# Attention inputs of a four-layer graph network as single 32-row products of blocks of 8 by 16 nodes

## The chip, the core and the metric

One NeuronCore of a Trainium2 chip. The time is device microseconds of one execution, median of the runs; all data are float32 and start and end in the chip's memory (HBM).

## What is computed

128 graphs of 64 nodes with 128 features, and a weighted, sparse adjacency `adj` (128, 64, 64), pass through four layers, each with a layer norm and relu ahead and a residual. Layer 0 is a filter network over all pairs; layers 2 and 3 are graph convolutions. The change touches layer 1, hyperbolic attention over all 64 x 64 pairs of a graph, cut here to what matters:

```python
h = proj(mobius_add(proj(mobius_matvec(W, x)), hyp_bias))
x_loc  = clip(logmap(h[:, :, None, :], h[:, None, :, :]), -1000, 1000)   # (b, i, j, d)
x_self = logmap(h, h)
q = concatenate([broadcast(x_self over j), x_loc], axis=-1)
a = silu(q @ att_w1.T + att_b1)
adj_att = sigmoid(a @ att_w2.T + att_b2)[..., 0]                         # (b, i, j)
support = sum over j of adj_att[..., None] * x_loc * mask[..., None]
t = concatenate([x_self, support], axis=-1)
out = silu(t @ mlp_w1.T + mlp_b1) @ mlp_w2.T + mlp_b2 + x_self           # then expmap, logmap0, silu, expmap0
```

`logmap(h_i, h_j)` is a combination of h_i and h_j with two scalars per pair. So what goes into the silu for a pair (i, j) is, per feature, V(i,j) times row j of one projection of h, plus U(i,j) times row i of the same projection, plus row i of another one. These are the three pair terms.

## The kernel before

Three stages follow one another with a barrier of all engines between them: set-up, the filter stage (layer 0) and the flow stage (layers 1 to 3). Nodes lie on partitions, two graphs to a tile of 128 nodes; eight tiles make a group, and there are eight groups.

The flow stage is software-pipelined by hand. Time is counted in slots of 64 ticks; `run` (line 760) emits each engine's instructions by the tick that is written beside each step. In slot s the attention of group s is done, one set of 2048 pairs every two ticks, a tile every eight. Beside it run four chains: `lead` (group s+2: layer 0's output, layer norm, hyperbolic map), `pair` (group s+1: the scalars U, VT and VP of all pairs, and the projections), `mix` (group s-1: sum over neighbours and the rest of layer 1) and `last` (group s-2: layers 2 and 3). All engines take their instructions strictly in order, so a wait holds up all that stands behind it on that engine.

A set in attention:
- `inputs(s)` on PE (lines 997 to 1015): for each of four blocks c, which are row groups of 32 partitions and write PSUM bank c, a product of 512 columns with `HW` (the projected rows of 32 nodes j) against `VD`, then one with `OWN` (two projections of 16 nodes i) against `UD`, added in the same bank. Every float32 matmul shows as two loads and two passes in the trace. Before block 0 PE waits for the first silu of the set before, before block 2 for the second.
- two silus on ACT (`silu`, line 1164), each over two banks, into `SI`.
- `dots(s)` on PE (line 1017): the product with `att_w2`, emitted one set behind, into bank 7. After 32 sets ACT's `weights` makes the group's attention of them.

Where the right sides come from: `VD` is made by POOL (`neighbours`, line 1318), half a tile at a time into three buffers, as VT spread over a mask. `UD` holds U on a block diagonal and ones; it lies in HBM in templates, made in set-up and copied 15 times in the filter stage; SP stores U of a group into it with 8 DMAs (line 946) and loads it for each tile.

SP issues all DMAs, in one order. `load_rows(tile)` (line 898, at ticks 1, 9, 17, ... for the tile after the present one) waits until the tile before the present one is through and issues 7 DMAs: 1 `HW`, 4 `OWN`, 2 `UD`, into two buffers. At tick 9 of `mix` (line 950) it loads the adjacency and `fH`, waits for the attention, stores it, waits for the store, and loads it back as 8 DMAs into `fat` (line 965). At tick 33 of `pair` (line 935) it stores the projections: 1 DMA to `hw` and 16 to `own`. At tick 49 it stores U. `last` and `lead` have some more at ticks 33 and 9. On DVE, `lead` may centre the next group (`bXC`, tick 35.9) only after those stores are through.

## Time and profile before

| | us |
|---|---|
| median of 3 runs (2820.68 to 2827.33) | 2826.15 |
| the profiled execution, its own time | 2826.92 |
| its span, first to last instruction | 2824.9 |
| PE busy, matmul (share of the span) | 2575.6 (91%) |
| DVE busy | 2198.6 (78%) |
| ACT busy | 2162.7 (77%) |
| POOL busy | 1704.4 (60%) |
| DMA, mean rate | 155 GB/s |

The filter stage takes the first half of the span, the flow stage the second; its slots last 132 to 152 us. Rows of the trace give start and length of an instruction, or of several of one kind that lie together (x8). Matmuls overlap, so their lengths don't add up: how far apart they begin is what counts. SP's DMA rows are the time in which SP issues, not the transfer.

### The profile page before, as it was taken

How to read it: one execution, taken by the hardware profiler on the slowest of the kernel's cores; microseconds unless marked ns; L12 is line 12 of the kernel's file. 1: busy time of each engine (PE TensorE's matmuls, PEld its weight loads, DVE VectorE, ACT ScalarE, POOL GpSimd, SP SyncE). 2: the span in 40 equal slices, each digit the busy share in tenths (PEclk: the TensorE clock that was granted, in tenths of full speed). 3: DMA queues.
4: the chain of work that ended last, by engine and by line, in shares of the span. 5: the costliest groups of instructions: out<-in, count | busy, mean ns of one | idle time of the engine just before them, and what ended most of it. 6: DMA issues, size and time to landing. Idle time of an engine off the chain costs nothing. (4 is left out here: it accounts for less than half of the span.)

```text
span 2824.9 us, 53482 instructions
## 1 busy us (share of the span) xinstructions
PE 2575.6 (91%) x21008; PEld 1077.0 (38%) x21008; DVE 2198.6 (78%) x3639; ACT 2162.7 (77%) x2136; POOL 1704.4 (60%) x773
## 2 busy tenths in 40 slices
PE   4899999999999999999962999999999999999963
PEld 2333333333333333333332334344443435343433
DVE  6698998989989899898978365768687878774356
...
GB/s 235 183 224 245 237 255 247 205 196 202 196 196 202 194 199 202 195 198 197 180 38 70 96 126 131 106 115 115 116 123 127 117 118 126 116 120 109 94 45 19
DMA packets 247241, 438.99 MB, mean 155 GB/s; under 512 B 86752, under 2 KB 212320, under 8 KB 213344
## 3 DMA queue, kind: packets, MB, share of 16 engines
...
## 5 line engine op out<-in xcount | busy, mean ns | idle before, releaser
L691 POOL TENSOR_TENSOR f_gate<-rfT,f_sq 128x1024 f32<-128x1024 f32 x512 | 1218.3, 2380 | 226.6 <-DVE f_prod L706 151.6
L624 PE MATMUL PS<-f_h,w_W2T 64*64 64x512 f32 x8192 | 998.4, 591 | 9.7 <-PE PS L624 1.9
L706 DVE SCALAR_TENSOR_TENSOR f_prod<-PS,b2l,f_gate 128x1024 f32<-128x1024 f32 x512 | 657.3, 1284 | 146.3 <-PE PS L624 110.4
L1164 ACT ACTIVATE a_silu<-PS,c_att_b 128x1024 f32<-128x1024 f32 x512 | 543.1, 1110 | 247.3 <-PE PS L1012 246.5
L586 ACT ACTIVATE f_h<-PS,c_b 128x1024 f32<-128x1024 f32 x512 | 556.6, 1113 | 166.6 <-PE PS L606 165.9
L698 DVE TENSOR_REDUCE yT<-f_prod 128x16 f32<-128x1024 f32 x512 | 618.7, 1209 | 0.0
L1324 POOL TENSOR_TENSOR a_vd<-n_vt,jmask 128x1024 f32<-128x1024 f32 x128 | 255.9, 2000 | 543.2 <-PE PS L1012 543.2
L624 PEld LDWEIGHTS PS<-f_h,w_W2T 64*64 64x64 f32 x8192 | 340.5, 133 | 561.4 <-issue 435.9
L606 PE MATMUL PS<-f_gauss,W1two 64*64 64x512 f32 x4096 | 545.8, 594 | 7.4 <-ACT f_gauss L573 4.8
L1008 PE MATMUL PS<-a_vd,a_hw 32*128 32x512 f32 x2048 | 397.6, 656 | 52.0 <-ACT a_silu L1164 24.8
L1012 PE MATMUL PS<-a_ud,a_own 32*128 32x512 f32 x2048 | 367.9, 603 | 0.0
L1027 PE MATMUL PS<-a_silu,w2sel 128*32 128x512 f32 x2048 | 278.0, 615 | 19.3 <-ACT a_att L1170 18.3
L606 PEld LDWEIGHTS PS<-f_gauss,W1two 64*64 64x64 f32 x4096 | 170.0, 133 | 287.5 <-issue 276.1
L568 ACT ACTIVATE f_gauss<-f_gauss,c_off 128x2048 f32<-128x2048 f32 x126 | 252.2, 2002 | 0.0
L573 ACT ACTIVATE f_gauss<-f_gauss 128x2048 f32<-128x2048 f32 x128 | 237.6, 1904 | 0.7
L1008 PEld LDWEIGHTS PS<-a_vd,a_hw 32*128 32x128 f32 x2048 | 127.1, 187 | 239.5 <-ACT a_silu L1164 127.7
L1012 PEld LDWEIGHTS PS<-a_ud,a_own 32*128 32x128 f32 x2048 | 155.3, 190 | 102.5 <-issue 97.6
L1027 PEld LDWEIGHTS PS<-a_silu,w2sel 128*32 128x32 f32 x2048 | 40.5, 108 | 193.8 <-issue 164.5
L573 ACT ACT_TABLE_LOAD x64 | 82.1, 1283 | 5.9 <-PEq L138 4.7
L586 ACT ACT_TABLE_LOAD x64 | 82.1, 1283 | 1.2
L1411 DVE TENSOR_TENSOR b_small<-b_small 128x8 f32<-128x8 f32 (+1 forms) x272 | 76.2, 280 | 8.3
L1283 ACT ACTIVATE f_lh<-f_x,g_small 128x128 f32<-128x128 f32 x128 | 52.1, 484 | 28.6 <-DVE g_small L1411 28.6
...
## 6 DMA issues: line engine op xcount, KB each, us to landing
f_gauss<-in_adj SPq DMA_DIRECT2D x128, 1024.0 KB, 11.7
f_sq<-adj_sq SPq DMA_DIRECT2D x256, 512.0 KB, 10.0
a_ud<-ud_d SPq DMA_DIRECT2D x128, 512.0 KB, 6.3
a_own<-own_d SPq DMA_DIRECT2D x256, 64.0 KB, 1.9
...
```

The lines of the kernel that those rows point to most:

```text
L573: A.activation(half_of(tile, h), half_of(tile, h), ACT.Exp, scale=COEFF).then_inc(s_gauss, 1)
L586: A.activation(H[n % H_BUFS][:], pre(n % 2), ACT.Softplus, bias=cols["b1"][:]).then_inc(s_ssp, 1)
L606: PE.matmul(pre(done % 2)[r, b, :], W1two[rows[b], r], G[tile % G_BUFS][rows[b], part * BANK:(part + 1) * BANK], start=True, stop=True).th ...
L624: PE.matmul(post("message", c)[rows[b], n, :], W2T[rows[k], rows[fh]], hidden(c, n)[rows[k], b, :], start=not second, stop=bool(second)).t ...
L691: GP.tensor_tensor(by_pair(GATE[c % GATE_BUFS][:]), rf, by_pair(squares), ALU.mult).then_inc(s_gate, 1)
L698: V.tensor_reduce(yT[:, fh, first:first + CHUNK // NODES], by_pair(PR[c % PR_BUFS][:]), AX, ALU.add).then_inc(s_sum, 1)
L706: V.scalar_tensor_tensor(PR[c % PR_BUFS][:], post("message", c).rearrange("p b n -> p (b n)"), b2l[:, c % 2:c % 2 + 1], GATE[c % GATE_BUFS ...
L1008: PE.matmul(PS[:, c, :], HW[n][rows_of(c), :], VD[s // 2 % VD_BUFS][rows_of(c), i % 2 * BANK:(i % 2 + 1) * BANK], start=True, stop=False)
L1012: last = PE.matmul(PS[:, c, :], OWN[n][rows_of(c), i, :], UD[n][rows_of(c), i * BANK:(i + 1) * BANK], start=False, stop=True)
L1027: last = PE.matmul(PS[part:part + 32, Z_BANK, :], w2sel[:, 32 - lane:64 - lane], SI[(2 * s + c // 2) % SI_BUFS][:, c % 2 * BANK:(c % 2 + 1 ...
L1164: A.activation(SI[p % SI_BUFS][:], PS[:, first:first + 2, :].rearrange("p b n -> p (b n)"), ACT.Silu, bias=cols["att_b1"][:]).then_inc(s_s ...
L1324: GP.tensor_tensor(VD[part % VD_BUFS][:].rearrange("p (i m) -> p i m", m=32), VT[tile // GT % 2][:, tile % GT, k * 2 * BLOCK:(k + 1) * 2 * ...
```

## The change

A set still has 2048 pairs, but a block of 32 partitions now covers all three pair terms at once, for 8 nodes i by 16 nodes j: 16 rows of projected j, 8 rows of the first projection of i and 8 of the second. So the two products of 512 columns per block become four products of 128 columns with no addition in PSUM, each with its own weights (`ROWS`), 16 matmuls per set for 8. The right side, `OUTER`, is made by POOL in two instructions per set out of two tables in SBUF, `BY_I` (by node i: VT, or fixed masks) and `BY_J` (by node j: U, or fixed masks), two sets ahead in four buffers. Each group's VT and U go straight from SBUF into these tables, with 8 and 32 DMAs. The rows of a tile come with 16 DMAs (8 of them broadcast j rows) in place of 7; the projections are stored with 4 DMAs of 512 KB in place of 17; the attention comes back with 16 DMAs in place of 8. The templates, their store in set-up and 15 copies in the filter stage go. Four activations at the start of the flow stage write the masks into the tables. Some tiles of `mix` and `last` now lie in `yT`. DVE's and PE's waits follow the new counts. The core of the diff:

```diff
@@ -553,9 +546,6 @@
                     load_squares(n)
-            if COPIES_FROM <= tile < COPIES_FROM + len(templates) - 1:
-                SP.dma_start(templates[tile - COPIES_FROM + 1], templates[0]).then_inc(s_copied, 16)
-        SP.wait_ge(s_copied, 16 * (len(templates) - 1))
         SP.wait_ge(d_later, 16 * LATER_WEIGHTS)
...
@@ -720,7 +710,8 @@
 N_FIRST, N_BANKS, Z_BANK = 4, 3, 7
-SI_BUFS, VD_BUFS, RING = 4, 3, 2
+SI_BUFS, OUTER_BUFS, OUTER_AHEAD = 4, 4, 2
+A_BLOCKS = NODES // A_BLOCK
 HALF_GT = GT // 2
...
@@ -794,24 +785,25 @@
     number = fill_numbers()
-    HW = [sb(f"a_hw{n}", [P, P]) for n in range(2)]
-    OWN = [sb(f"a_own{n}", [P, BLOCKS, P]) for n in range(2)]
-    UD = [sb(f"a_ud{n}", [P, PAIRS // 2]) for n in range(2)]
-    VD = [sb(f"a_vd{n}", [P, CHUNK]) for n in range(VD_BUFS)]
+    ROWS = [sb(f"a_rows{n}", [P, A_BLOCKS, 2, P]) for n in range(2)]
+    BY_I = [sb(f"a_by_i{n}", [P, 2, GT, NODES]) for n in range(2)]
+    BY_J = [sb(f"a_by_j{n}", [P, GT, A_BLOCKS, 2, BLOCK]) for n in range(2)]
+    OUTER = [sb(f"a_outer{n}", [P, 2, BLOCK, BLOCK]) for n in range(OUTER_BUFS)]
     SI = [sb(f"a_silu{n}", [P, CHUNK]) for n in range(SI_BUFS)]
     VP = [sb(f"n_vp{n}", [P, GT, NODES]) for n in range(3)]
-    VT = [sb(f"n_vt{n}", [P, GT, NODES]) for n in range(2)]
+    VT = sb("n_vt", [P, GT, NODES])
-    fXC, fSQ, fH, fST, fUU, fAV, fBT, gH, gU = (sb("f_" + n, [P, GT, P]) for n in
-                                               ("xc", "sq", "h", "st", "uu", "av", "abt", "lh", "lu"))
-    fat, fam, ftm = (sb("f_p" + n, [P, GT, NODES]) for n in ("at", "am", "tm"))
+    fXC, fSQ, fH, fST, fUU, fAV, fBT = (sb("f_" + n, [P, GT, P]) for n in ("xc", "sq", "h", "st", "uu", "av", "abt"))
+    gH, gU = (yT[:, n, 0:GT * P].rearrange("p (t d) -> p t d", d=P) for n in range(2))
+    fam = sb("f_pam", [P, GT, NODES])
+    fat, ftm = (yT[:, n, GT * P:GT * P + GT * NODES].rearrange("p (t d) -> p t d", d=NODES) for n in range(2))
     BS, FS = sb("b_small", [P, len(B_ROWS), GT]), sb("f_small", [P, len(F_ROWS), GT])
...
@@ -899,17 +898,17 @@
             if tl == 0:
-                SP.wait_ge(d_hw, (g + 1) * 16)
-                SP.wait_ge(d_own, (g + 1) * 16 * 16)
-                SP.wait_ge(d_u[g % 2], (g // 2 + 1) * 8 * 16)
-            SP.dma_start(HW[n][:], d["hw"][tile * P:(tile + 1) * P, :]).then_inc(s_rows[n], 16)
+                SP.wait_ge(d_hw, (g + 1) * 64)
+            graphs = d["hw"][:, tile * P:(tile + 1) * P, :, :]
+            by_j = graphs[0, :, 0, :].rearrange("(c j m) d -> c m j d", c=4, j=2)
+            by_i = graphs.rearrange("u (b c i) n d -> u b i c (n d)", b=2, i=A_BLOCK)
             for c in range(4):
-                SP.dma_start(OWN[n][rows_of(c), :, :],
-                             d["own"][2 * tile + c // 2].rearrange("i u n d -> (u n) i d")).then_inc(s_rows[n], 16)
-            for h in range(2):
-                SP.dma_start(UD[n][h * NODES:(h + 1) * NODES, :],
-                             d["ud"][g % RING, h, 2 * tl:2 * tl + 2].rearrange("j p c -> (j p) c")
-                             ).then_inc(s_rows[n], 16)
+                for j in range(2):
+                    SP.dma_start(ROWS[n][rows_by_j(c), :, j, :],
+                                 by_j[c, :, j].unsqueeze(1).broadcast_to([BLOCK, A_BLOCKS, P])).then_inc(s_rows[n], 16)
+                for part in range(2):
+                    SP.dma_start(ROWS[n][rows_by_i(c, part), :, :, :].rearrange("p c n d -> p c (n d)"),
+                                 by_i[part, c // 2]).then_inc(s_rows[n], 16)
 
...
@@ -932,20 +931,24 @@
             taken(SP, number["pair", g, "r3"])
-            SP.dma_start(d["hw_t"][:, nodes, :], bXC[:]).then_inc(d_hw, 16)
             for u, buf in enumerate((bXC, bSQ)):
-                for h in range(2):
-                    for i in range(BLOCKS):
-                        SP.dma_start(d["own"].rearrange("(t b) i u n d -> b i u n t d", b=2)[h, i, u][:, nodes, :],
-                                     buf[block_of(i, h)]).then_inc(d_own, 16)
+                for n in range(2):
+                    SP.dma_start(d["hw_t"][u][n][:, nodes, :], buf[:]).then_inc(d_hw, 16)
             yield 49
+            SP.wait_ge(b["vt"], g + 1)
+            before(SP, s_outer, (g - 1) * SLOT_SETS * 2)
+            if g == 0:
+                SP.wait_ge(s_fixed, 4)
+            for c in range(4):
+                for j in range(2):
+                    SP.dma_start(BY_I[g % 2][rows_by_j(c), j, :, :], VT[block_of(c % 2 * 2 + j, c // 2), :, :]
+                                 ).then_inc(d_vt[g % 2], 16)
             SP.wait_ge(b["U"], g + 1)
-            for h in range(2):
-                for i in range(BLOCKS):
-                    first = (g % RING * 2 + h) * 2 * GT * 32 * 4 * BANK + i * BANK
-                    SP.dma_start(bass.AP(d["ud"].tensor, first, [[4 * BANK + 32, BLOCK], [32 * 4 * BANK, 2 * GT], [1, 32]]),
-                                 U[g % 3][block_of(i, h)].rearrange("p t (j m) -> p (t j) m", m=32)
-                                 ).then_inc(d_u[g % 2], 16)
+            for c in range(4):
+                for i in range(A_BLOCKS):
+                    first = c // 2 * NODES + i * A_BLOCK
+                    SP.dma_start(BY_J[g % 2][rows_by_i(c, 0), :, i, :, :].rearrange("p t j m -> p t (j m)"),
+                                 U[g % 3][first:first + A_BLOCK, :, c % 2 * 32:c % 2 * 32 + 32]).then_inc(d_u[g % 2], 16)
 
...
@@ -959,11 +962,11 @@
             SP.wait_ge(d_att, (g + 1) * 16)
-            att = d["att"][g].rearrange("(c h r) (n m) -> c h n r m", h=2, r=2 * GT, n=BLOCK)
+            att = d["att"][g].rearrange("(h j c t) (n m) -> h c j n t m", h=2, j=2, c=BLOCKS, n=BLOCK)
             for h in range(2):
                 for i in range(BLOCKS):
-                    SP.dma_start(fat[block_of(i, h)].rearrange("p t (j m) -> p (t j) m", m=32),
-                                 att[2 * h + i % 2, i // 2]).then_inc(d_atin, 16)
+                    for jb in range(2):
+                        SP.dma_start(fat[block_of(i, h), :, jb * 32:(jb + 1) * 32], att[h, i, jb]).then_inc(d_atin, 16)
             yield 33.1875
...
@@ -998,21 +1001,19 @@
             if k == 0:
-                PE.wait_ge(s_rows[n], (tile // 2 + 1) * 7 * 16)
-            if k % 2 == 0:
-                PE.wait_ge(s_vd, s // 2 + 1)
-            for c in range(4):
-                i = k ^ (c % 2)
-                if c % 2 == 0:
-                    before(PE, s_silu, 2 * s + c // 2 - 1)
-                PE.matmul(PS[:, c, :], HW[n][rows_of(c), :],
-                          VD[s // 2 % VD_BUFS][rows_of(c), i % 2 * BANK:(i % 2 + 1) * BANK], start=True, stop=False)
-            for c in range(4):
-                i = k ^ (c % 2)
-                last = PE.matmul(PS[:, c, :], OWN[n][rows_of(c), i, :], UD[n][rows_of(c), i * BANK:(i + 1) * BANK],
-                                 start=False, stop=True)
-                if c % 2:
-                    last.then_inc(s_pair, 1)
+                PE.wait_ge(s_rows[n], (tile // 2 + 1) * 16 * 16)
+            PE.wait_ge(s_outer, 2 * s + 2)
+            for j in range(2):
+                for u in range(2):
+                    for c in range(4):
+                        if j == 0 and u == 0 and c % 2 == 0:
+                            before(PE, s_silu, 2 * s + c // 2 - 1)
+                        first = (2 * j + u) * P
+                        last = PE.matmul(PS[:, c, first:first + P], ROWS[n][rows_of(c), 2 * k + u, j, :],
+                                         OUTER[s % OUTER_BUFS][rows_of(c), j, u * A_BLOCK:(u + 1) * A_BLOCK, :]
+                                         .rearrange("p a m -> p (a m)"), start=True, stop=True)
+                        if j and u and c % 2:
+                            last.then_inc(s_pair, 1)
 
...
@@ -1020,13 +1021,12 @@
             PE.wait_ge(s_silu, 2 * s + 2)
-            for c in range(4):
-                i = k ^ (c % 2)
-                part = 32 * (2 * (c // 2) + i % 2)
-                lane = i // 2 * 2 * GT + 2 * tl + c % 2
-                last = PE.matmul(PS[part:part + 32, Z_BANK, :], w2sel[:, 32 - lane:64 - lane],
-                                 SI[(2 * s + c // 2) % SI_BUFS][:, c % 2 * BANK:(c % 2 + 1) * BANK],
-                                 start=head, stop=True, skip_group_check=True)
+            for b in range(2):
+                for jb in range(2):
+                    part, lane = 32 * (2 * b + jb), k * GT + tl
+                    last = PE.matmul(PS[part:part + 32, Z_BANK, :], w2sel[:, 32 - lane:64 - lane],
+                                     SI[(2 * s + b) % SI_BUFS][:, jb * BANK:(jb + 1) * BANK],
+                                     start=head, stop=True, skip_group_check=True)
             last.then_inc(s_dot, 1)
...
@@ -1155,6 +1155,11 @@
         A.activation(norm[:, 3:4], norm[:, 1:2], ACT.Tanh).then_inc(s_hb, 1)
+        for n in range(2):
+            A.activation(BY_I[n][:].rearrange("p j t (c a) -> p (j t c) a", a=A_BLOCK),
+                         by_a[:].unsqueeze(1).broadcast_to([P, 2 * GT * A_BLOCKS, A_BLOCK]), ACT.Copy).then_inc(s_fixed, 1)
+            A.activation(BY_J[n][:].rearrange("p t c j m -> p (t c j) m"),
+                         by_m[:].unsqueeze(1).broadcast_to([P, 2 * GT * A_BLOCKS, BLOCK]), ACT.Copy).then_inc(s_fixed, 1)
         own_p = Order(o_pa)
...
@@ -1315,16 +1321,19 @@
 
-        def neighbours(part):
-            tile, k = part // 2, part % 2
-            before(GP, s_pair, (part - VD_BUFS + 1) * 4)
-            if tile % GT == 0 and k == 0:
-                GP.wait_ge(b["vt"], tile // GT + 1)
-            shape = [P, 2 * BLOCK, 32]
-            GP.tensor_tensor(VD[part % VD_BUFS][:].rearrange("p (i m) -> p i m", m=32),
-                             VT[tile // GT % 2][:, tile % GT, k * 2 * BLOCK:(k + 1) * 2 * BLOCK].unsqueeze(2)
-                             .broadcast_to(shape),
-                             jmask[:].unsqueeze(1).broadcast_to(shape), ALU.mult).then_inc(s_vd, 1)
+        def outer(s):
+            g, tl, k = s // SLOT_SETS, s // 4 % GT, s % 4
+            if s % SLOT_SETS == 0:
+                GP.wait_ge(d_vt[g % 2], (g // 2 + 1) * 8 * 16)
+                GP.wait_ge(d_u[g % 2], (g // 2 + 1) * 32 * 16)
+            before(GP, s_pair, (s - OUTER_BUFS + 1) * 2)
+            shape = [P, 2, A_BLOCK, BLOCK]
+            for u in range(2):
+                GP.tensor_tensor(OUTER[s % OUTER_BUFS][:, :, u * A_BLOCK:(u + 1) * A_BLOCK, :],
+                                 BY_I[g % 2][:, :, tl, (2 * k + u) * A_BLOCK:(2 * k + u + 1) * A_BLOCK]
+                                 .unsqueeze(3).broadcast_to(shape),
+                                 BY_J[g % 2][:, tl, 2 * k + u, :, :].unsqueeze(2).broadcast_to(shape), ALU.mult
+                                 ).then_inc(s_outer, 1)
 
```

## Rows read from the trace of the kernel before

**Rows 1.** The page, part 1: busy time and share of the span, instructions
```profile
PE 2575.6 (91%) x21008; PEld 1077.0 (38%) x21008; DVE 2198.6 (78%) x3639; ACT 2162.7 (77%) x2136; POOL 1704.4 (60%) x773
```

**Rows 2.** Busy time of each engine in one slot of the middle
```profile
2139.30:2286.00 146.70, 142.61 (x1040) 64.37 (x1040) 116.80 (x303) 113.91 (x144) 60.58 (x32) 0.99 0.52 121
```

**Rows 3.** Timeline of ACT and PE over bare sets: start us, us, what, [idle before]
```profile
1570.37 2.12 ACT L1164 ACTIVATE a_silu<-PS,c_att_b 128x1024 f32<-128x1024 f32 x2 [1.62 <-PE PS L1012]
1567.34 1.07 PE L1027 MATMUL PS<-a_silu,w2sel 128*32 128x512 f32 x8
...
1570.72 1.07 PE L1027 MATMUL PS<-a_silu,w2sel 128*32 128x512 f32 x8
...
1574.45 1.06 PE L1027 MATMUL PS<-a_silu,w2sel 128*32 128x512 f32 x8
```

**Rows 4.** Timeline of PE and PEld, then single passes: ns min/median/max
```profile
1992.26 0.31 PEld L1008 LDWEIGHTS PS<-a_vd,a_hw 32*128 32x128 f32 x8 [0.84 <-issue]
...
2169.76 1.16 PE L1041 MATMUL PS<-f_abt,f_lh 128*128 128x128 f32 x8
...
2171.81 1.04 PE L1012 MATMUL PS<-a_ud,a_own 32*128 32x512 f32 x8
...
L1008 PE MATMUL PS<-a_vd,a_hw x8: 587/640/692, 2003.3 to 2004.1; 32*128 32x512 f32 x8
...
L1041 PE MATMUL PS<-f_abt,f_lh x8: 275/275/377, 2169.8 to 2170.6; 128*128 128x128 f32 x8
```

**Rows 5.** Timeline of SP after the first tile of a slot
```profile
2148.72 0.34 SPq L905 DMA_DIRECT2D a_hw<-hw_d  x1
2149.11 1.86 SPq L907 DMA_DIRECT2D a_own<-own_d  x4
...
2164.66 3.76 SPq L965 DMA_DIRECT2D f_pat<-att_d  x8
2168.46 0.45 SPq L905 DMA_DIRECT2D a_hw<-hw_d  x1
```

**Rows 6.** The same, ahead of the next slot
```profile
2241.48 0.35 SPq L905 DMA_DIRECT2D a_hw<-hw_d  x1
...
2245.77 4.63 SPq L946 DMA_DIRECT2D ud_d<-n_u  x8
```

**Rows 7.** POOL by shape, mean ns of one; then timeline of POOL and DVE
```profile
L1324 POOL TENSOR_TENSOR a_vd<-n_vt,jmask 128x1024 f32<-128x1024 f32 x128 | 255.9, 2000 | 543.2 <-PE PS L1012 543.2
...
L1348 POOL TENSOR_TENSOR b_pden<-b_py,b_small 128x512 f32<-128x512 f32 x8 | 8.3, 1042 | 25.8 <-ACT b_poy L1175 25.8
...
2005.66 1.91 POOL L1324 TENSOR_TENSOR a_vd<-n_vt,jmask 128x1024 f32<-128x1024 f32 x1 [5.17 <-PE PS L1012]
...
2005.67 1.93 DVE L1405 TENSOR_SCALAR g_small<-g_small 128x16 f32<-128x16 f32 x1
```

**Rows 8.** Waits in the slot: us in total, times, longest
```profile
POOL a_vd L1324 <- PE PS L1012: 68.1, 14, 10.1
...
DVE f_pat L1407 <- DMA f_pat<-att_d: 3.2, 1, 3.2
```

**Rows 9.** The page, part 6: DMA issues, KB each, us to landing
```profile
a_own<-own_d SPq DMA_DIRECT2D x256, 64.0 KB, 1.9
```

**Rows 10.** Timeline of PE: first pass of tile 3 and of the next slot
```profile
2184.06 1.16 PE L1008 MATMUL PS<-a_vd,a_hw 32*128 32x512 f32 x8
...
2277.78 1.61 PE L1008 MATMUL PS<-a_vd,a_hw 32*128 32x512 f32 x6
```

**Rows 11.** Timeline of SP in the middle of the slot: first own stores
```profile
2204.11 7.86 SPq L939 DMA_DIRECT2D own_d<-b_xc  x8
```

**Rows 12.** Timeline of SP and PE where attention begins
```profile
1539.82 3.79 SPq L946 DMA_DIRECT2D ud_d<-n_u  x8
...
1554.47 1.23 PE L1008 MATMUL PS<-a_vd,a_hw 32*128 32x512 f32 x4 [24.76 <-DMA a_ud<-ud_d]
```

**Rows 13.** Busy time, clock granted, DMA share and GB/s after a PE idle
```profile
2286.90:2290.30 3.40, 3.40 (x20) 1.00 (x16) 3.33 (x3) 0.84 (x2) 3.40 (x2) 0.56 0.01 4
```

93 lines of the change are left out of this document (46 added, 47 removed).

## The prediction

> **What bounds the kernel now.** The page's engine line has PE at 91% [rows 1], which says little: a row of PE ends late, by the model. So I cut the attention part into its slots (one group of 16 graphs each) and took one in the middle, 146.7 us long: PE busy 142.6, DVE 116.8, ACT 113.9, POOL 60.6 [rows 2]. DVE and ACT have some 30 us of room in it, PE almost none.
>
> The timeline of PE and ACT shows what a bare set (2048 pairs) is made of [rows 3]. ACT does two silus in 2.12 us, then sits idle for the pair products, 1.62 us in the row; the dots begin at 1567.34, 1570.72 and 1574.45, so a set takes 3.38 or 3.74, 3.56 on average. It is a loop: the products may overwrite their banks only after the silus, the silus wait for the products. In it each of the two products per block is four concurrent row groups of two passes. A row of eight passes lasts 1.04 us and one pass 0.59, so the second four begin 0.43 later [rows 4]: 0.86 per product, 1.72 per set for both. Dots take another 1.0.
>
> The third reader is SP, the one queue that issues every DMA. The page doesn't count it as busy. The timeline of SP has 1.86 us for four, 3.76 for eight: 0.475 to 0.49 us each, whatever their size up to some 128 rows [rows 5, 6]. Per tile it issues 7 now.
>
> **The change, part by part.**
>
> *Pair products.* Two products of 512 columns become four of 128 per row group, each with its own weight load. The nearest row is a burst of eight passes of 128 columns with their own loads: 1.16 us in all, the first pass 0.377, the others 0.275, so one begins every 0.111 us [rows 4]. That burst is one row group of 128 rows; here four groups of 32 go side by side. Loads of four groups do run side by side now: eight loads, two for each of the four groups, fit into 0.31 us [rows 4]. So inputs cost 4 x 2 x 0.111 = 0.89 per set for 1.72: 0.83 less PE. Where ACT and PE take turns, the gain is smaller, since blocks 2 and 3 still wait for the second silu and everything behind them in the queue with them: ACT's gap becomes about 0.1 (wake-up, load) + 6 x 0.111 + 0.2 (end to ACT) = 1.0, and a bare set 3.15 for 3.56, 0.41 less. Sets with matmuls of the other chains gain up to 0.83; sets where ACT has much of its own to do behind the silus gain nearly nothing. I take 2.7 us per ordinary tile of four sets, 1.5 to 2.2 for tiles full of ACT work, bounds 0 and 3.3. If nothing else bound, a full slot would lose 16 us.
>
> *A rule against it.* The first pass of a product has 0.692 us on record and later ones 0.587: 0.105 us is the exposed load [rows 4]. The burst of 128-column passes shows no such gap after its first pass, though its loads all go to the same rows. The Trainium skill ("TensorE: Matmul & The Clock Gate", Part 3) says under what overlaps and what doesn't that a weight load overlaps matmuls in flight only when its row group differs (an earlier part of the page also allows a background buffer); by that rule every short pass here would show its load. The trace disagrees for 128 rows, and nothing in it shows a 32-row group. What it would do is rival C.
>
> *POOL.* 128 instructions of 128x1024 (2.00 us each [rows 7]) become 512 of 128x256. 128x512 costs 1.04 at the least [rows 7], so 256 elements are 0.52 to 0.75 us, 1.0 to 1.5 per set for 1.0 now. Hidden: POOL waits for PE 68 us per slot [rows 8]. Its long instructions hold up DVE (a 128x16 operation took 1.93 us beside a 1.91 us one [rows 7]); shorter ones shorten each hold and make more of them: 0, bounds -5 and +5 per slot. Two sets of lead instead of two to four: 0.
>
> *SP, per tile.* 16 DMAs for 7: 7.6 us of issue for about 3.5. With 1.9 us for the last to land [rows 9], rows are there 9.1 us after SP starts; a tile lasts 14 to 22, so alone it is hidden. It isn't where other DMAs share the queue; three stretches of a full slot:
> - After tile 0 (SP starts tile 2's rows at 2148.72 and tile 3's at 2168.46). Between them 3.42 us of rows and 16.3 of others, 3.76 of it for 8 attention loads [rows 5]. These become 16: 20.2. Tile 3 can start at 7.6 + 20.2 + 9.1 = 36.9 after 2148.72. It starts after 35.3 now (2184.06 [rows 10]). So three tiles take 1.6 us more, where PE alone would take 6 less.
> - Before the next slot. SP starts the last tile's rows at 2241.48, then 8 stores of U in 4.63 [rows 6]. The change has 8 + 32 = 40 DMAs there, 19.8 us. The next group's rows follow: 7.6 + 19.8 + 9.1 = 36.5. PE starts the next slot 36.3 after 2241.48 now (2277.78 [rows 10]). So no gain here.
> - In between, hw and own stores (1 + 16 DMAs; the first eight of own take 7.86 us with stalls [rows 11], the other eight 3.8, 12.3 with hw's) become 4 of 512 KB. I take 8 us, landing 2 to 3 later than now because the rows ahead take 4.2 more. DVE's next centring waits for them, and ACT and PE for it: 1.5 us given back.
>
> Full slot: +1.6 +0.2, and the other four tiles -8.4 (2.2, 2.7, 1.5 and 2.0) + 1.5, so -5.1; five such slots, -25.5. By the same terms the first, which has no attention loads, gives -12, the seventh, with no new group to centre, -6, the last, with no stores of U, -12: -55.5 in all for attention.
>
> *Given back elsewhere.* Attention's start: PE sat idle 24.76 us until its first rows landed, SP storing U at 1539.82 and PE starting at 1554.47 [rows 12]. With 40 DMAs, 16 rows' DMAs and 1.9 us it is 19.8 + 7.6 + 1.9 = 29.3 for 14.7: +14. Tail: the last group's attention loads are 8 more of 0.47 to 0.49 us, with nothing beside them, +4. Clock: behind the slot's end, where PE stands idle for a moment, it ran 3.4 us at a granted clock of 0.56, mostly the lower level, 1.2 GHz [rows 13]; the wait ahead of tile 3 in seven slots is some 7 us, and makes such a stretch: 1.5 each, +10. DVE: attention weights and the adjacency arrive 4 to 8 us later in each slot (it waits 3.2 for the weights now [rows 8]) and DVE has 30 us of room, some of it needed again by later chains: +12, bounds 0 and +45. Set-up and filter stage lose a 1 MB store and 15 copies, with PE busy throughout: -1, bounds -4 and 0. Four activations at attention's start fall where ACT is idle: 0.
>
> Sum: -55.5 + 14 + 4 + 10 + 12 - 1 = -16.5. The profiled execution took 2826.9 (span 2824.9, 2.0 around it), the median is 2826.15: 2810.
>
> **Rivals.**
> A, SP has room after all (broadcast rows issue faster than 0.475 us, or its stretches overlap otherwise). Then PE's gain arrives: 16 in seven slots, 18 in the first, -130; with start and tail half of the above, 2826 - 130 + 9 + 10 = 2715. For: outside the three stretches SP is idle for most of a tile. Against: 0.475 us holds over all small DMAs seen.
> B, slower: DVE reaches U too late. U was done before SP asked for it (SP started the stores at once, at 2245.77 [rows 6]). In the changed order SP asks after rows and 8 DMAs of VT, 11.5 us after 2241.48. From 8 us more lag on, each us delays the 32 loads, rows and the slot. DVE's longer waits (4 to 8 us in the first stretch, 2 to 3 in the middle) could give 15: 7 us too late, seven times, +49: 2860.
> C, slower: loads of short passes aren't hidden, by the rule above. A pass is 0.111 + 0.105, inputs 8 x 0.216 = 1.73, no gain on PE. The stretches still add 1.8 per slot, +13, start, tail, clock and DVE +40: 2880.
> That the change does nothing measurable is the forecast's own upper part, gains and returns cancelling.
>
> **How the numbers follow.** Forecast 0.40 (own range 2775 to 2840), A 0.20, B 0.27, C 0.10, rest 0.03. The range 2735 to 2885 leaves out more than half of A (2700 to 2735) and the upper part of B and C, about 2 in 10. A measurement tells 0.3%, 8.5 us, from no change. Faster by more: 0.27 of the forecast and A, 0.47. Same: 0.10 of the forecast, 0.04 of B: 0.14. Slower: 0.03 of the forecast, 0.23 of B, 0.10 of C, 0.03 of the rest: 0.39.
>
> **What the profile will show.** Pair-product passes 0.11 apart within a row group (0.22 is C). ACT's gap 1.0 in bare sets. POOL instructions of 0.5 to 0.75 us. SP: 7.6 us per tile, 20 in the burst for U and VT; PE waiting for a DMA of rows at tile 3 and at each slot's start. If the slot is near 131 us, A; if SP waits for DVE's U before the burst, B. The largest risk is DVE's lag, which I only bounded.

## The result and the profile after

The changed kernel takes 2943.1 us (median of 4 runs, 2942.6 to 2947.2) where the kernel before took 2823.4 in the same session: a ratio of 1.0427, 95% interval 1.0407 to 1.0448, slower by 120 us. The forecast was 2810 and its range ended at 2885. PE's share fell from 91% [rows 1] to 82%, page, part 1 and a line of part 2:

```profile
PE 2418.9 (82%) x25104; PEld 1176.0 (40%) x25104; DVE 2180.2 (74%) x3641; ACT 2166.5 (74%) x2140; POOL 1784.1 (61%) x1157
...
PEclk8999999999999999999866988798989989888976
```

Where the time went is a matter of the first pass of each tile on PE. The first tile starts at 1582.03 for 1554.47 [rows 12], +27.5; from there to the last tile it is 1224.9 us for 1133.4, +91.5; behind it +1.2. Slots and tiles are counted from 0 here. A slot of the middle (slot 4), cut at the same tiles in both kernels (busy time of each engine; behind the engines the granted clock, DMA share, GB/s):

```profile
2203.60:2259.00 55.40, 42.96 (x590) 26.04 (x590) 37.62 (x106) 38.03 (x49) 30.94 (x32) 0.87 0.56 105
2259.00:2317.40 58.40, 53.66 (x615) 34.13 (x616) 46.23 (x99) 47.39 (x63) 24.13 (x29) 0.93 0.59 127
2317.40:2362.60 45.20, 28.55 (x353) 17.16 (x352) 30.15 (x98) 28.40 (x31) 15.00 (x18) 0.81 0.35 61
```

Tiles 0 to 2 took 53.0 us before, 3 to 5 took 60.4, and 6 and 7 took 33.3. So +2.4, -2.0 and +11.9: the loss sits in front of the next slot. The timeline of SP, PE and POOL there, against [rows 6] (at the front of slot 4):

```profile
2153.83 0.78 SPq L907 DMA_DIRECT2D a_rows<-hw_d  x2
...
2160.74 5.02 SPq L944 DMA_DIRECT2D a_by_i<-n_vt  x8
2165.81 24.43 SPq L950 DMA_DIRECT2D a_by_j<-n_u  x32
2190.34 0.86 SPq L907 DMA_DIRECT2D a_rows<-hw_d  x2
...
2203.56 2.09 PE L1012 MATMUL PS<-a_outer,a_rows 32*128 32x128 f32 x32 [14.51 <-DMA a_rows<-hw_d]
...
2191.55 1.19 POOL L1332 TENSOR_TENSOR a_outer<-a_by_i,a_by_j 128x256 f32<-128x256 f32 x2 [16.71 <-DMA a_by_j<-n_u]
```

SP hands over V and U in 29.6 us (2160.74 to 2190.34), 0.63 us for each DMA of V and 0.76 for each of U (0.73 to 0.76 over the eight bursts), and then begins the next slot's rows; PE starts on them 13.2 us later, having been idle for 14.5. The same two prices make the start of attention, 42.0 us for 14.7:

```profile
1540.05 5.01 SPq L944 DMA_DIRECT2D a_by_i<-n_vt  x8
1545.11 23.50 SPq L950 DMA_DIRECT2D a_by_j<-n_u  x32
1568.65 0.92 SPq L907 DMA_DIRECT2D a_rows<-hw_d  x2
...
1582.03 2.09 PE L1012 MATMUL PS<-a_outer,a_rows 32*128 32x128 f32 x32 [51.54 <-DMA a_rows<-hw_d]
```

Behind tile 0 the stretch of [rows 5] is this, 39.5 us from the rows of tile 2 to tile 3 on PE, 35.3 before:

```profile
2219.51 0.78 SPq L907 DMA_DIRECT2D a_rows<-hw_d  x2
...
2238.35 7.42 SPq L969 DMA_DIRECT2D yT<-att_d  x16
2245.81 0.90 SPq L907 DMA_DIRECT2D a_rows<-hw_d  x2
...
2258.99 2.09 PE L1012 MATMUL PS<-a_outer,a_rows 32*128 32x128 f32 x32 [4.68 <-DMA a_rows<-hw_d]
```

Over the execution these waits sum up so (us in all, times, longest); 51.5 and 26.2 of them are the ones at attention's start:

```profile
PE PS L1012 <- DMA a_rows<-hw_d: 199.6, 15, 51.5
POOL a_outer L1332 <- DMA a_by_j<-n_u: 139.3, 8, 26.2
```

In bare sets the products did what they were predicted to do. In sets of the kind of [rows 3] one set of dots begins 3.19 us after the other (2184.79, 2187.98; 3.15 predicted), ACT is idle for 0.97 to 1.07 us ahead of its silus (1.0 predicted), and the passes of one row group lie 0.11 apart, as in [rows 4] (seven passes of each of four groups in 1.16 us, the first one 0.37 long):

```profile
2182.79 0.49 PE L1012 MATMUL PS<-a_outer,a_rows 32*128 32x128 f32 x4
2183.70 1.16 PE L1012 MATMUL PS<-a_outer,a_rows 32*128 32x128 f32 x28 [0.42 <-ACT a_silu L1169]
2184.79 1.07 PE L1027 MATMUL PS<-a_silu,w2sel 128*32 128x512 f32 x8
...
2187.98 1.07 PE L1027 MATMUL PS<-a_silu,w2sel 128*32 128x512 f32 x8
```

### The profile page after: what moved, and what is told of

It is laid out like the page before. It is cut to its first block and busy times, and to the rows that moved or that the text cites. A ratio compares the mean times of both kernels' runs of the same rounds, so it can differ in the third digit from the quotient of the medians.

```text
span 2945.1 us, 62968 instructions
## 1 busy us (share of the span) xinstructions
PE 2418.9 (82%) x25104; PEld 1176.0 (40%) x25104; DVE 2180.2 (74%) x3641; ACT 2166.5 (74%) x2140; POOL 1784.1 (61%) x1157
## 5 line engine op out<-in xcount | busy, mean ns | idle before, releaser
L1332 POOL TENSOR_TENSOR a_outer<-a_by_i,a_by_j 128x256 f32<-128x256 f32 x512 | 347.7, 701 | 681.9 <-PE PS L1012 542.6
L1012 PE MATMUL PS<-a_outer,a_rows 32*128 32x128 f32 x8192 | 412.7, 312 | 297.5 <-DMA a_rows<-hw_d 199.6
L1012 PEld LDWEIGHTS PS<-a_outer,a_rows 32*128 32x128 f32 x8192 | 337.7, 210 | 478.3 <-DMA a_rows<-hw_d 210.3
L1027 PE MATMUL PS<-a_silu,w2sel 128*32 128x512 f32 x2048 | 311.1, 682 | 24.1 <-ACT a_att L1175 22.2
L1414 DVE TENSOR_SCALAR b_small<-b_small 128x8 f32<-128x8 f32 (+1 forms) x104 | 21.0, 202 | 80.3 <-ACT b_small L1210 58.1
L1420 DVE TENSOR_TENSOR f_small<-f_small 128x8 f32<-128x8 f32 x208 | 67.6, 325 | 9.3 <-ACT f_small L1264 3.5
L1289 ACT ACTIVATE yT<-f_x,g_small 128x128 f32<-128x128 f32 x128 | 52.2, 483 | 29.4 <-DVE g_small L1420 29.3
L1027 PEld LDWEIGHTS PS<-a_silu,w2sel 128*32 128x32 f32 x2048 | 42.5, 114 | 68.7 <-ACT a_att L1175 23.5
L1420 DVE TENSOR_TENSOR f_h<-f_h,f_uu 128x1024 f32<-128x1024 f32 x8 | 12.2, 1524 | 73.4 <-POOL f_uu L1395 73.4
```

The lines of the kernel that those rows point to most:

```text
L1012: last = PE.matmul(PS[:, c, first:first + P], ROWS[n][rows_of(c), 2 * k + u, j, :], OUTER[s % OUTER_BUFS][rows_of(c), j, u * A_BLOCK:(u + ...
L1027: last = PE.matmul(PS[part:part + 32, Z_BANK, :], w2sel[:, 32 - lane:64 - lane], SI[(2 * s + b) % SI_BUFS][:, jb * BANK:(jb + 1) * BANK], ...
L1332: GP.tensor_tensor(OUTER[s % OUTER_BUFS][:, :, u * A_BLOCK:(u + 1) * A_BLOCK, :], BY_I[g % 2][:, :, tl, (2 * k + u) * A_BLOCK:(2 * k + u + ...
```

## The experiments

The theory from these rows (T): what counts is SP's in-order queue, and in it the price of the 40 small DMAs and the landing of 1 MB of rows per tile. Its rivals: L, the rows' landing alone counts and the burst lies beside it; P, the products, POOL or DVE set the time. Each ratio is to the kernel before in the same session, which took 2822.9 to 2827.5 us there.

| run | what it is | us | ratio to before, 95% |
|---|---|---|---|
| no_burst | V, U moved for groups 0, 1 only | 2861.6 | 1.0131 (1.0108 to 1.0154) |
| rows_once | rows moved for tiles 0, 1 only | 2796.2 | 0.9900 (0.9884 to 0.9917) |
| no_small | both left out, attention weights back in 1 DMA | 2771.0 | 0.9813 (0.9793 to 0.9833) |
| before_no_small | the same left out of the kernel before | 2812.4 | 0.9959 (0.9945 to 0.9974) |
| b_burst | kernel before, 32 small DMAs more | 2899.9 | 1.0273 (1.0257 to 1.0288) |
| price | U's 32 DMAs in another form per group, one profiled execution | 2906.5 | |
| dram | V, U by DRAM, 10 DMAs for 40 | 2828.1 | 1.0009 (0.9997 to 1.0021) |
| att2 | weights back in 4 DMAs for 16 | 2891.3 | 1.0241 (1.0225 to 1.0256) |
| v2 | both of these | 2779.3 | 0.9852 (0.9836 to 0.9868) |
| rows16 | own rows by 16 partitions | 2858.3 | 1.0126 (1.0112 to 1.0140) |
| lead4 | no_small, POOL four sets ahead, V and U for group 0 only | 2772.2 | 0.9819 (0.9803 to 0.9834) |
| v3 | v2, POOL's f_x behind f_uu | 2780.8 | 0.9859 (0.9837 to 0.9882) |
| no_small_pads | no_small, long fillers on PE | 2842.6 | 1.0064 (1.0050 to 1.0077) |
| v2_pads | v2, long fillers | 2842.3 | 1.0059 (1.0046 to 1.0073) |
| no_small_pads2 | no_small, short fillers | 2763.8 | 0.9777 (0.9763 to 0.9792) |
| v2_pads2 | v2, short fillers | 2766.4 | 0.9787 (0.9772 to 0.9803) |
| v4_pads | v2_pads2 and rows16 | 2738.5 | 0.9697 (0.9683 to 0.9710) |

### Take the transfers away

```diff
             yield 49
+            if g >= 2:
+                return
...
         def load_rows(tile):
+            if tile >= 2:
+                return
```

The first piece is no_burst, the second rows_once; POOL's and PE's waits follow them. no_small has both and reads the attention weights back in one DMA. In no_burst and no_small the 40 DMAs of groups 0 and 1 are still in.

> Leaves out the 40 small DMAs of V and U (the 8 of n_vt and the 32 of n_u) for groups 2 to 7, so the attention of those groups is computed from the tables of groups 0 and 1. Everything else stays, the 16 row DMAs per tile too. Theory T (the one in-order queue sets the slot: 29.6 us of burst, then rows that need 13.3 us): PE's wait of 14.5 us ahead of a slot and POOL's of 16.7 go in six slots, 6 x 14.5 = 87, so 2855 us, down to 2830 if DVE and ACT catch up too; the start of attention stays late (its burst is still there). Rival L (the lateness is in the landing of 1 MB of rows per tile, the burst lies beside it): the wait at the slot's end stays above 10 us, 2915 to 2943. Rival P (PE's short products, or DVE and POOL, set the time): 2943.

> Leaves out the 16 row DMAs of every tile from tile 2 on, so those tiles use the rows of tiles 0 and 1. The burst of 40 DMAs and the 16 attention reloads stay. Theory T: SP reaches the burst 6.2 us sooner and nothing follows it but its own landing, so the stretch ahead of the next slot falls from 48.3 to about 32, PE's wait there from 14.5 to about 0 to 3, and the wait ahead of tile 3 (5 us) goes: 7 x 12 + 7 x 5 = 119 less, 2825 us (2800 to 2850). Rival L: the same or more, 2800, and the burst itself gets shorter (below 25 us for 40) because no rows move beside it. Rival P: 2943.

> Leaves out both of the above, and reads the attention weights back in one DMA of 128 rows instead of 16 (values in another order). What is left is PE, ACT, POOL and DVE with the changed products. If the predicted gain on PE is there (inputs 0.83 us less per set, a full slot 16 us shorter than the kernel before), about 2700 us (2690 to 2730). Rival P (short products or POOL's and DVE's lateness cost the time): 2850 or more. In between: the gain on PE is partly eaten by DVE or ACT, whose share the slot's waits will show.

no_burst took 2861.6 us for T's 2855. PE's waits for rows, 199.6 us, are 115.8 without the burst, and from slot 2 on those ahead of a slot are gone; L said that they would stay above 10 us and the time at 2915 or more. rows_once took 2796.2: T's 2825 gave the rows too little, and the time alone would fit L's 2800. L's other sign did not come, a burst below 25 us without rows beside it: slot 4's lasts 29.0 (2217.58 to 2246.57), nearly as with them. So both parts count, in one queue: alone they bring 82 and 147 us, together (with the weights in one DMA) 172. P falls. With neither, 2771: the changed products are worth something, but 70 us less than the expected 2700. A part of it is the start, whose burst is still in. The rest is told by the kernel before, freed in the same way:

> The kernel before with the same left out as in the changed kernel without small transfers: rows only for tiles 0 and 1, U stored for group 0 only, attention weights back in one DMA (values in another order); hw and own stores stay. It gives the changed products their right comparison, with no transfer in the way of either. Theory G (the gain per set that I took is too large, 2.7 us per tile where the tiles show 1.3 to 1.6): this run near 2815 us (2805 to 2825) and the other at 2771, a gain of some 45 for the 130 of rival A. Theory H (the gain is there, but the kernel before is held by nothing but PE, and the changed one by something else without DMAs): also 2815, and the tiles tell: those full of DVE's and POOL's work (2 and 6) are longer after the change, the others shorter by 2.7. If this run falls to 2790 or less, transfers held the kernel before too, and the products gain 20 or less.

2812.4: transfers held it by 11 us only, and the changed kernel gains 41 us on it. By PE's timelines it loses 23.5 at attention's start (first tile at 1579.5 for 1556.0), where its burst is still in, and gains 66 from the first tile to the last, which is what compares with the 130 of rival A: 16.6 in slot 0 (18 predicted), where DVE and ACT are busy for 58 and 91 us of 118, 11.5 in slot 1, and 4.3 to 7.5 in slots 2 to 6. A middle slot of each without small transfers (no_small first, then before_no_small):

```profile
2107.30:2247.10 139.80, 121.10 (x1552) 74.21 (x1553) 111.71 (x303) 113.70 (x143) 70.29 (x79) 0.93 0.19 51
```

```profile
2125.50:2269.60 144.10, 140.12 (x1040) 63.66 (x1040) 119.71 (x303) 113.93 (x143) 59.30 (x32) 1.00 0.19 45
```

4.3 us a slot for the 16 predicted. By tile, from PE's timeline: 17.2, 15.0, 19.7, 14.0, 21.4, 18.4, 21.2, 12.9 after; 17.0, 16.3, 18.1, 17.3, 22.7, 19.4, 18.8, 14.5 before. Tiles 1, 4, 5 and 7 gain 1.0 to 1.6, tile 3 gains 3.3, tile 0 nothing, and tiles 2 and 6 lose 1.6 and 2.4. So G and H are each half right: the ordinary tile gains what G says and not the 2.7 of H, and the two tiles full of other work are longer, as H says. What PE waits for in the slot is short and many: in no_small 8.2 us for silus, 3.5 for the attention weights' activation, 3.2 for POOL's f_uu and 3.0 for DVE's f_x; in before_no_small 3.8 us in all.

### Put the burst into the kernel before

```diff
+            for c in range(4):
+                for i in range(8):
+                    first = c // 2 * NODES + i * 8
+                    SP.dma_start(d["sc"][g, c * 8 + i], U[g % 3][first:first + 8, :, c % 2 * 32:c % 2 * 32 + 32]
+                                 ).then_inc(d_u[g % 2], 16)
```

> The kernel before, all its work kept, with 32 more DMAs of U behind its 8 stores (SBUF to a DRAM scratch, 64 pieces of 128 bytes each, read by nobody; the next group's first rows wait for them as they do for the 8). One part of the change alone. Theory T (the burst in SP's queue is enough, whatever the products): 32 x 0.70 = 22.4 us more in the queue; the next slot's rows start at 2272.7 for 2261.2 in slot 4, PE some 5 to 12 us later per slot, seven times, and 22 at attention's start: 2823 + 22 + 60 = 2905 (2880 to 2925). Rival P (the burst only costs because the changed products or rows surround it): 2845 (start alone).

2899.9 for the 2905 expected, +77 us, with the old products, 21 of them at attention's start. The end of its slot 4:

```profile
2294.57 4.78 SPq L947 DMA_DIRECT2D ud_d<-n_u  x8
2299.39 22.75 SPq L953 DMA_DIRECT2D sc_d<-n_u  x32
2323.50 0.34 SPq L906 DMA_DIRECT2D a_hw<-hw_d  x1
...
2333.11 2.09 PE L1014 MATMUL PS<-a_vd,a_hw 32*128 32x512 f32 x8 [5.81 <-DMA a_ud<-ud_d]
```

The burst alone costs two thirds of what the whole change did. It isn't quite alone: SP waits here for all 40 DMAs to land ahead of the next rows (1.4 us, 2322.14 to 2323.50), where the kernel before waits for its 8 and the changed one leaves the wait to POOL.

### The price of one small DMA

```diff
-                    SP.dma_start(BY_J[g % 2][rows_by_i(c, 0), :, i, :, :].rearrange("p t j m -> p t (j m)"),
-                                 U[g % 3][first:first + A_BLOCK, :, c % 2 * 32:c % 2 * 32 + 32]).then_inc(d_u[g % 2], 16)
+                    SP.dma_start(to, fro).then_inc(d_u[g % 2], 16)
```

> The 32 DMAs of U in the burst get another form in each group, 64 pieces of 128 bytes or 8 KB each: groups 0 and 1 as they are (SBUF to SBUF, 8 partitions by 8 pieces), 2 SBUF to DRAM in the same pieces, 3 DRAM to SBUF in the same pieces, 4 SBUF to SBUF as 8 pieces of 1 KB, 5 SBUF to SBUF as 64 partitions by one piece of 128 bytes, 6 DRAM to SBUF as 8 pieces of 1 KB, 7 SBUF to DRAM as 8 pieces of 1 KB. Groups 2 to 7 compute with other values in their tables. Rival F (the form sets the price on SP's queue): 0.73 to 0.77 us each where both ends are in SBUF and the pieces are 128 bytes, 0.47 to 0.49 in the others. Rival D (the queue stalls because the DMA engines are behind with the rows): about the same price in all groups, whatever the form.

SP's timeline, the 32 DMAs of U in groups 1 to 7, one line each:

```profile
1679.00 23.36 SPq L967 DMA_DIRECT2D a_by_j<-n_u  x32
...
1835.61 23.33 SPq L967 DMA_DIRECT2D sc_d<-n_u  x32
...
1999.25 22.10 SPq L967 DMA_DIRECT2D a_by_j<-sc_d  x32
...
2160.58 22.32 SPq L967 DMA_DIRECT2D a_by_j<-n_u  x32
...
2317.90 20.90 SPq L967 DMA_DIRECT2D a_by_j<-n_u  x32
...
2477.87 11.29 SPq L967 DMA_DIRECT2D a_by_j<-sc_d  x32
...
2623.30 11.44 SPq L967 DMA_DIRECT2D sc_d<-n_u  x32
```

8 KB each time: 0.73 us as the change has them (0.73 to 0.76 in the eight bursts of the changed kernel), 0.73 and 0.69 with one end in DRAM and the same 64 pieces of 128 bytes, 0.70 with both ends in SBUF and 8 pieces of 1 KB, 0.65 for 64 partitions by one piece, and 0.35 to 0.36 for 8 pieces of 1 KB with one end in DRAM. So the form does set the price, by a factor of two, but not as F put it: of these 8 KB DMAs only those in 1 KB pieces with an end in DRAM are cheap. Nor is it the pieces alone: the stores of [rows 12], 16 partitions by 16 pieces of 128 bytes, took 0.47 each. What rule gives 0.73 for 8 partitions and 0.47 for 16 was not found. The engines behind were not what held SP: in the seven stretches the DMA engines' share is 0.06 to 0.14, as low in the dear groups as in the cheap ones. D falls. Each form was tried in one group of one execution.

### Fewer DMAs

```diff
+            SP.dma_start(d["vt"][g], VT[:]).then_inc(d_out_vt, 16)
+            SP.dma_start(d["un"][g], U[g % 3][:]).then_inc(d_out_u, 16)
...
+            for c in range(4):
+                SP.dma_start(BY_I[g % 2][rows_by_j(c), :, :, :].rearrange("p j t n -> p j (t n)"), vt_rows[c]
+                             ).then_inc(d_vt[g % 2], 16)
...
+                SP.dma_start(BY_J[g % 2][rows_by_i(c, 0), :, :, :, :].rearrange("p t i j m -> p t i (j m)"),
+                             u_rows[c // 2, c % 2]).then_inc(d_u[g % 2], 16)
...
-                    part, lane = 32 * (2 * b + jb), k * GT + tl
+                    part, lane = 32 * (2 * b + jb), tl * BLOCKS + k
...
+                for jb in range(2):
+                    SP.dma_start(fat[h * NODES:(h + 1) * NODES, :, jb * 32:(jb + 1) * 32], att[h, jb]).then_inc(d_atin, 16)
```

The first three pieces are from dram, the last two from att2; v2 has both.

> Same computation as the changed kernel, but V and U go to DRAM in one store each and come back in 4 loads each: 10 DMAs in the place of 40, the same number of 128-byte pieces for U. Theory T (the price is per DMA on SP's queue, 0.63 to 0.77 us each): the burst falls from 29.6 to about 8 us, two landings of 2 us included; the stretch ahead of the next slot becomes 6 + 8 + 13 = 27, below two tiles of PE, so 14.5 to 17 us per slot go, seven times, and some 20 at attention's start: 2943 - 112 - 20 = 2811 (2790 to 2840). Rival L (the pieces of 128 bytes and the rows fill the DMA engines whatever the number of DMAs): the burst lands as late as before, 2920 to 2943.

> The changed kernel with the attention weights read back in 4 DMAs of 64 rows by 8 pieces in the place of 16 (the dots put their lanes in the order tile, quarter, so that the rows merge); same computation. Theory T (every DMA costs SP's queue 0.48 us there): the block between the rows of tile 2 and of tile 3 falls from 26.3 to 20.5 us, tile 3 starts 5.8 us sooner in seven slots: 2943 - 41 = 2902 (2895 to 2915). Rival L (the time is in the pieces moved, whose number is the same, or PE has no use for it because DVE is late): 2930 to 2943.

> V and U by DRAM (10 DMAs for 40) and the attention weights in 4 DMAs for 16, together; same computation. Theory T: the two savings lie in different stretches and add up: 2828 - 41 = 2787 (2775 to 2805), faster than the kernel before by 1 to 1.7%. If DVE's and POOL's lateness in tiles 5 and 6 takes part of it back: 2800 to 2815. Rival L: 2828.

dram came out at 2828.1 (2811 expected), att2 at 2891.3 (2902, its range from 2895), v2 at 2779.3 (2787). L falls here too: the pieces of U are as many as before, only the DMAs are fewer. In v2 the burst lasts 9.2 us for 29.6, the wait for both stores included. U's four loads still go to 8 partitions each and cost 0.71 us apiece; it is their number that fell:

```profile
2222.66 0.35 SPq L945 DMA_DIRECT2D vt_d<-n_vt  x1
2223.06 0.67 SPq L947 DMA_DIRECT2D un_d<-n_u  x1
2227.26 1.72 SPq L951 DMA_DIRECT2D a_by_i<-vt_d  x4
2229.02 2.83 SPq L956 DMA_DIRECT2D a_by_j<-un_d  x4
```

Each cure alone leaves the other stretch late; both together make the change worth having, 1.5% faster than the kernel before.

### The landing of the rows

```diff
-        hw_d = dram("hw_d", [2, GRAPHS * NODES, 2, P])
+        hw_d = dram("hw_d", [GRAPHS * NODES, 2, 2, P])
...
-                for part in range(2):
-                    SP.dma_start(ROWS[n][rows_by_i(c, part), :, :, :].rearrange("p c n d -> p c (n d)"),
-                                 by_i[part, c // 2]).then_inc(s_rows[n], 16)
+                SP.dma_start(ROWS[n][rows_by_i(c), :, :, :].rearrange("p c n d -> p c (n d)"),
+                             by_i[c // 2]).then_inc(s_rows[n], 16)
```

> The changed kernel with its own rows (hw and own by i) brought in 16 partitions at a time in place of twice 8: the DRAM array keeps the two kinds beside each other per node, the rows of a block go in the order node, kind; 12 DMAs per tile for 16, same bytes, same computation, burst and attention reloads unchanged. In the changed kernel a tile's rows land 13.2 us after SP begins them, at 110 GB/s and a DMA share of 0.66 with nothing else moving. Theory E (a DMA of 8 partitions is served by only 8 of the 16 DMA engines, as a page has it, so half of the bytes queue up): 12 DMAs take 4.7 us of issue and the rows land some 7.5 us after SP begins; the wait at the slot's end falls from 14.5 to 8.8, the 4.7 at tile 3 goes: 2943 - 7 x 10.4 - 6 = 2865 us (2850 to 2885). Rival C (only the count of DMAs matters, 4 fewer at 0.38): 1.5 us per stretch, 15 stretches, 2920 us (2910 to 2930).

2858.3: theory E's 2865, not its rival's 2920, though the rows are there after 9.8 us and not the 7.5 that E took. In the changed kernel little but rows moves from 2190.3 to 2203.5, 1.45 MB at 110 GB/s: the tile's own 1 MB and, from 2196.59 on, a part of the next tile's. The DMA share is 0.66. With 16 partitions it is 0.92, and 1.30 MB move in the 9.8 us from SP's start to PE's (a row of after, then of rows16). The share is rough: for 2153.4 to 2158.5 of rows16 alone it reads 1.20.

```profile
2190.30:2203.50 13.20, 0.00 (x0) 0.00 (x0) 8.49 (x19) 4.12 (x4) 7.94 (x9) 0.55 0.66 110
```

```profile
2148.70:2158.50 9.80, 0.62 (x8) 0.00 (x0) 5.28 (x11) 3.80 (x4) 7.94 (x9) 0.76 0.92 133
```

The Trainium skill ("DMA: Bandwidth & Descriptors", Why a DMA increments its semaphore by 16 and not by 1) says that a DMA is spread over the largest number of engines up to 16 that divides the slowest dimension of both its ends, so 8 partitions get 8 engines. The two shares agree with it, and so do the packets of the price run: there are 277 packets of 4 bytes in the stretch with 32 DMAs of 8 partitions by 1 KB, and 512 in that with 32 DMAs of 64 partitions, 8 to 9 and 16 to a DMA. Which engines were idle no row here shows.

### The gain of the products

```diff
-SI_BUFS, OUTER_BUFS, OUTER_AHEAD = 4, 4, 2
+SI_BUFS, OUTER_BUFS, OUTER_AHEAD = 4, 6, 4
...
         def last(g):
-            yield 20
+            yield 20.125
```

The first is lead4, the second, in POOL's program, v3. To make room, lead4 also has one pair of tables for two and moves V and U for group 0 alone.

> Like the run without the small transfers (all slots work with the tables of group 0, the rows of tiles 0 and 1, attention weights in one DMA), but POOL makes its outer products four sets ahead in six buffers, for two sets in four. That run was at 2771 us, its full slot at 139.9 us where the prediction's PE side alone gives 131; PE waited 7.1 us per slot for POOL's outer products and 3.2 for f_uu, which stands behind outer products in POOL's queue. Theory Q (the short lead costs it): 4 to 7 us less per slot, 2720 to 2740 us. Theory G (PE's gain per set is simply smaller beside ACT's other work): 2765 to 2775.

> The version with V, U and attention weights in few DMAs, and one more edit: POOL adds the last bias (f_x, 2.8 us) behind the product f_uu and not ahead of it. In tile 2 of the run without small transfers PE waited 3.2 us for f_uu, after that addition. Theory H (POOL's serial work now comes late for the faster PE): 2 to 2.8 us per slot, seven times: 2760 to 2766. If it only moves the wait: 2779.

2772.2 and 2780.8: neither POOL's short lead (Q) nor the place of one long POOL instruction costs anything that the end feels. The clock costs a little. Tile 6 of no_small's slot, then PE's timeline in it:

```profile
2213.00:2234.20 21.20, 18.41 (x193) 11.55 (x192) 18.63 (x71) 17.81 (x20) 7.19 (x10) 0.76 0.01 3
```

```profile
2214.06 1.07 PE L1028 MATMUL PS<-a_silu,w2sel 128*32 128x512 f32 x8
...
2220.85 1.13 PE L1042 MATMUL PS<-yT,f_av 128*128 128x128 f32 x8 [1.27 <-DVE f_x L1817]
2223.18 2.99 PE L1013 MATMUL PS<-a_outer,a_rows 32*128 32x128 f32 x32 [1.21 <-ACT a_silu L1170]
2226.11 1.94 PE L1028 MATMUL PS<-a_silu,w2sel 128*32 128x512 f32 x8
```

Behind two idle moments of 1.27 and 1.21 us the granted clock is at half, 1.2 GHz, for 10 us; inputs of a set take 2.99 us there for 1.17, its dots 1.94 for 1.07. In this slot 4 PE stood at the lower level for 20.5 us in all, in the changed kernel's for 39.6, in before_no_small's never; over slots 0 to 6 it is 146 us in no_small and 31 in before_no_small. To see what that costs, PE was given work for its waits, products into the PSUM bank that the next product overwrites (with the counts of v2_pads2; the calls ahead of `u0` are left out):

```diff
+PADS = {3: 14, 42: 12}
...
+            free(n)
+            for _ in range(count):
+                PE.matmul(bank(n)[:, 0, :], ident[:], ident[:], start=True, stop=True)
```

> The changed kernel without small transfers (2771 us), with extra 128x128 products on TensorE in front of its waits: 30 ahead of the first dots of a slot, 18 ahead of u0, 22 and 9 ahead of the set inputs at ticks 42 and 52, 5 ahead of e0; each writes the PSUM bank that the next product overwrites, so the computation is that run's. In that run one full slot had 20.5 us at TensorE's lower clock, always behind idle stretches of 1.2 to 3.5 us (the kernel before without small transfers: none); a set's inputs took 2.99 us there for 1.17, its dots 1.94 for 1.07. Theory K (a faster TensorE idles, falls to 1.2 GHz and gives the gain back): the clock column shows under 5 us at the lower clock in a slot, and the slot is 3 to 7 us shorter, 2720 to 2750 us. Rival N (the sets at the lower clock were waiting for ACT and DVE anyhow): clock up, time 2765 to 2775. Rival W (the extra products only delay): above 2775.

These fillers, 30 products and not 14 ahead of a slot's first dots, were too long: 6.96 us in a wait of 3.46, and some waited for a bank themselves. At 2842.6 (and v2_pads, with the same ones, at 2842.3) rival W came true, the fillers delay, and nothing is told on K. Cut to the waits:

> The last test of the clock had fillers that were too long: each product is two passes (60 passes, 6.96 us, where the wait was 3.46), and those ahead of e0 and at tick 52 stood 5 us for a PSUM bank. Here only 14 products (28 passes, 3.1 us) ahead of the first dots of a slot, where TensorE waits 3.46, and 12 ahead of u0, where it waits 3.16. Theory K: the 6.8 and 3.4 us at the lower clock behind these two are gone, 1.5 to 3 us per slot, 2750 to 2762 us for 2771. Rival N: clock up, 2767 to 2775.

> The version with few DMAs (2779 us) with fillers cut to the waits they fill: 14 products ahead of the first dots, 8 ahead of u0 (wait 2.27), 12 at tick 42 (wait 3.45). Of 17.1 us at the lower clock in slot 4 some 3.4 remain. Theory K: 3 to 5 us less per slot, 2745 to 2760 us. Rival N: 2775 to 2783.

2763.8 for 2771.0, the ratio to before going from 0.9813 to 0.9777, and 2766.4 for 2779.3, from 0.9852 to 0.9787: by the ratios 10 and 18 us. The first step is hardly more than the intervals, the second is clear of them. Of v2's 17.1 us at the lower level in slot 4, 3.4 are left. So K holds in part, at 1.5 and 2.6 us a slot where 1.5 to 3 and 3 to 5 were expected; both times lie between the ranges of K and N. The first dots of v2_pads2's slot (in v2 they took 1.93 us behind a 3.46 wait):

```profile
2105.11 3.39 PE L1160 MATMUL PS<-ident 128*128 128x128 f32 x28
2108.64 1.07 PE L1033 MATMUL PS<-a_silu,w2sel 128*32 128x512 f32 x8
```

### All together

> V and U by DRAM, attention weights in 4 DMAs, own rows by 16 partitions and the short fillers (14 products ahead of the first dots, 8 ahead of u0, 12 at tick 42). Same computation as the reference. Without the edit of the rows it was 2766 us, and there no full slot waited for rows any more; only attention's start does: 6 us earlier, 2760 us (2750 to 2770).

2738.5 us, 3.0% faster than the kernel before and 22 better than expected. The expectation counted the rows at the start only; the ratio fell by 0.009 against v2_pads2, some 25 us, of which the start has 2.2; the most lies in the slots (slot 1 has 132.6 us for 138.7, slot 4 138.6 for 140.4). PE's waits for rows fell from 36.8 us, five of them and four in the slots, to the one of 26.2 at the start. So the premise that no slot waited for rows any more was not so; what the rest of the 25 us is was not taken apart.

## Why the prediction was wrong

It named the right mechanism (SP's queue takes the gain back) and the right three places, and was 133 us off, to the other side of no change, because its sizes were. The two that count most come first.

- *The burst*, "8 + 32 = 40 DMAs there, 19.8 us". Measured 29.6. The step that failed is the price of 0.475 to 0.49 us "whatever their size", read off row DMAs, stores and reloads of 16 to 128 partitions and taken for 8 partitions by 128-byte pieces from SBUF to SBUF, a form that the trace of before doesn't hold. It was the term with the largest count and had no bounds of its own. (Even at its own price the burst was 19.0 to 19.6 us.)
- *Rows there 9.1 us after SP starts* (7.6 + 1.9 is 9.5, as the start was counted). Measured 13.2, though SP needed less, 6.2 us for 16. The step that failed is the landing of 1.9 us, the median of single 64 KB DMAs of 32 partitions [rows 9]; here 1 MB has to land, half of it in 8-partition DMAs, with the next tile's rows behind it, and PE could start only 7.0 us after SP had issued the last of it. Ahead of a slot the two make 29.6 + 13.2 + 6.9 = 49.7 from the last tile's rows to PE for 36.5 predicted; that difference, seven times, is 92 us (slot 4's numbers taken for all seven).
- *Tile 3*, 36.9 predicted, 39.5 measured: the reloads came at 0.46 each, a little under the price taken, and what lies between the rows took 18.7 us for 20.2; rows again were late, 13.2 for 9.1.
- *The start*, +14 predicted, +27.5 measured, by the same two prices. *The tail*, +4 predicted, +1.2.
- *PE's gain*, 16 us for a full slot. The size for bare sets was right to 0.04 us; "2.7 us per ordinary tile" was not: with no transfer in the way four tiles gain 1.0 to 1.6, one 3.3, one nothing, and two lose. ACT is busy 113.7 of 139.8 us, and PE, 3.8 us in waits with the old products, has 17.9 with the new ones, for ACT, POOL and DVE. Rival A's 2715 took the same 16 us, and fails by the same step: SP out of the way is 2771.
- *The clock*, +10 us. Slot 4's lower-level time grew from 3.4 to 39.6 us; what filling some of the idle moments gives back is 10 to 18 us in kernels whose slots hold 14 to 31 us of it. How much of the 39.6 costs anything in the changed kernel, where PE waits for rows anyway, is open.
- *DVE's lag* (forecast +12, rival B 2860): within the slots SP never waited for U or V before the burst (once, 13.9 us, ahead of attention's start, where the kernel before waits 14.5 too). B's mechanism did not occur. Rival C's, 2880, the nearest number, didn't either: the passes are 0.11 apart, 0.22 only at the lower clock.
- *POOL* was right: 0.70 us on average for 256 elements, bounds 0.52 to 0.75, and its waits for PE in a slot stayed (69.8 us for 68.1 [rows 8]).

With the sizes as measured in the two stretches, at the start and in the tail, the same sum would have been 2810 + 7 x (49.7 - 36.5) + 7 x (39.5 - 36.9) + 13.5 - 3 = 2931. The 12 us left were not taken apart. PE's overrated gain alone would make more of them (tiles 3 to 6 of slot 4 took 0.8 us more than before, where 6.9 less were forecast), and the 12 us set down for DVE's lag would take some back; that the sum closes so nearly is partly luck.
